# A four-layer graph network on one core: the weighted layer's sorted scan of gathered rows replaced by dense weight matrices of 144 sources

## The reference

```
h = relu(layernorm(x));  x = x + edge_statistics(h, edge_attr_32)      # sums, maxima, means over src, two matmuls
h = relu(layernorm(x));  x = x + convolution(h)                        # sums of scaled h[src] over dst, one matmul
h = relu(layernorm(x))
w = where(src != dst, edge_weight, 0)
x = x + (1 + eps) * h + segment_sum(w[:, None] * h[dst], src)          # the weighted layer
h = relu(layernorm(x));  x = x + gated(h, edge_attr_64, src, dst)      # two rounds of a GRU
```

## Time and profile before

| | us |
|---|---|
| median of 3 runs | 6442.04 (6427.77 to 6444.42) |
| span of the profiled execution | 6441.6 |
| median of the runs less that span | 0.4 |
| PE busy | 3666.2 (57%), 27862 instructions |
| DVE busy | 4108.0 (64%), 11121 |
| ACT busy | 1238.9 (19%), 3929 |
| POOL busy | 3600.3 (56%), 3398 |
| mean granted TensorE clock | 0.685 |

### The profile page before, as it was taken

How to read it: one execution, slowest core, us unless ns; L and a number is a source line. 1 busy time by engine, 2 the same in 40 slices (tenths; PEclk the granted TensorE clock), 3 DMA queues, 4 the chain that set the end, 5 groups by cost and what they waited for, 6 DMA issues and landing times. The chain is left out here.

```text
span 6441.6 us, 115669 instructions
## 1 busy us (share of the span) xinstructions
PE 3666.2 (57%) x27862; PEld 2870.0 (45%) x27863; DVE 4108.0 (64%) x11121; ACT 1238.9 (19%) x3929; POOL 3600.3 (56%) x3398
## 2 busy tenths in 40 slices
PE   4377778778778778740017686554432222210988
PEld 3234555555555555530017686554432222210977
DVE  8888877777777777769630577775554444432333
ACT  0023444444444444420010000000000000000111
POOL 0025777777777777740230277777777777763000
PEclk5588887887888887865559655555555555555999
DMA  1001211211111211127509344443333233321977
GB/s 25 2 20 35 63 53 51 63 53 52 61 54 52 63 53 52 61 78 286 182 17 426 108 99 100 102 95 78 87 76 71 58 69 69 69 50 62 386 292 269
DMA packets 459644, 634.91 MB, mean 99 GB/s; under 512 B 342019, under 2 KB 397479, under 8 KB 426087
## 3 DMA queue, kind: packets, MB, share of 16 engines
q1 hardware_dynamic: 347202, 493.86, 23.4%
q0 software_dynamic: 106624, 86.11, 6.5%
q10 hardware_dynamic: 5670, 53.26, 2.2%
HBM read 420.15 MB, written 212.81 MB: 98 GB/s over the span
## 5 line engine op out<-in xcount | busy, mean ns | idle before, releaser
L414 POOL DMA_INDIRECT sorted_rows<-rows,place_i x1568 | 1813.7, 1157 | 801.3 <-issue 462.6
L1349 POOL DMA_INDIRECT gathered_rows<-feature_table,gather_index x1568 | 1579.3, 1007 | 501.5 <-issue 463.0
L1435 PE MATMUL block_total<-attr_half,block_hot 128*128 128x65 f32 x4048 | 876.2, 418 | 320.0 <-DMA attr_half<-in_edge_attr_dram 304.5
L1435 PEld LDWEIGHTS block_total<-attr_half,block_hot 128*128 128x128 f32 x4048 | 867.2, 332 | 329.0 <-issue 309.9
L595 PE MATMUL part<-high,low 128*128 x3520 | 916.8, 392 | 118.3 <-DVE high L466 109.7
L466 DVE TENSOR_TENSOR high<-iota_g,window_keys 128x1568 f16 x880 | 850.8, 967 | 0.3
L580 PE MATMUL count_rows<-counts,lo_rows_f 128*128 128x49 f32 x3136 | 718.5, 320 | 0.0
L1393 DVE TENSOR_SCALAR block_hot<-iota_f,block_keys 128x128 f32<-128x128 f32 x2024 | 502.7, 302 | 183.5 <-PE block_total L1435 61.4
L595 PEld LDWEIGHTS part<-high,low 128*128 x3520 | 379.6, 108 | 484.9 <-issue 347.9
L580 PEld LDWEIGHTS count_rows<-counts,lo_rows_f 128*128 128x128 f32 x3136 | 579.5, 230 | 25.2 <-issue 21.0
L1404 DVE TENSOR_TENSOR_SCAN gathered_rows<-same_src,sum_carry,gathered_rows 128x32 f32<-128x32 f32 x3136 | 578.2, 266 | 6.3
(11 more groups left out here) (352 smaller groups left out, 5510.7 us busy)
## 6 DMA issues: line engine op xcount, KB each, us to landing
piece_round<-slabs SPq DMA_DIRECT2D x98, 1568.0 KB, 9.1
slabs<-slab SPq DMA_DIRECT2D x49, 1568.0 KB
piece_conv<-slabs SPq DMA_DIRECT2D x49, 1568.0 KB, 23.0
attr_half<-in_edge_attr_dram SPq DMA_DIRECT2D x184, 352.0 KB
scanned<-scan_out ACTq DMA_DIRECT2D x8, 6272.0 KB, 29.7
scanned<-gathered_rows SPq DMA_DIRECT2D x49, 1024.0 KB, 5.1
scan_rows<-sorted_rows SPq DMA_DIRECT2D x8, 3430.0 KB, 29.6
sorted_rows<-rows,place_i POOLq DMA_INDIRECT x1568
```

The lines of the kernel that those rows point to most:

```text
L414: pool.indirect_dma_start(sorted_rows[:, :], bass.IndirectOffsetOnAxis(ap=place_i[:, h, u:u + 1], axis=0), rows[:, h, u, :], None).then_in ...
L1349: pool.indirect_dma_start(got[b][:, j, :], None, table[:, :], bass.IndirectOffsetOnAxis(ap=index[b][:, j:j + 1], axis=0)).then_inc(gathere ...
L1435: nc.tensor.matmul(total[b][:, :], hot[:, j, :], attr[j // HALF][:, j % HALF, :], start=False, stop=True, skip_group_check=True).then_inc( ...
```

## The change

`sdw` and the sorted rows get a fourth column: src, a key, dst's low seven bits, and the weight, which is set to 0 where src equals dst. The key is made by fifteen more DVE operations in `prepare_keys`. `scan_sorted` drops its three operations for `dst_sorted` and `w_sorted`, and ACT copies the last three columns to `edge_records` in DRAM, sorted by source, 12 bytes per edge. `find_ranges` drops the blocks of 128 targets. Under the first layer, `edge_statistics_layer` writes the starts of the runs to DRAM, reads them back by group, and works out a plan: one pass per 128 edges of the fullest window of a group, with the first record of each window (`pass_index`) and the key base (`pass_base`) of each pass.

The table, the 1568 gathers and the 2024 one-hot products of the attributes go. In their place:

The core of the new code (in this order: the order of passes; ScalarE; VectorE; TensorE):

```diff
+        def passes(engine, name, body, between=None):
+            body(0, 0, None, 0)
+            body(1, 1, None, 1)
+            with engine.Fori(0, SCANS) as i:
+                for b in range(2):
+                    body(2 * i + 2 + b, b, 2 * i + b, 2)
+            if between is not None:
+                between()
+            count = one_value(nc, g["pass_count"][0:1, 0:1], name, LEAST, MOST)
+            with engine.Fori(SCANS, count) as i:
+                for b in range(2):
+                    body(2 * i + 2 + b, b, None, 2)
...
+            def second(q, b, j):
+                act.wait_ge(equal_ready, q * NBATCH + j + 1)
+                for w in range(GB):
+                    last = nc.scalar.mul(low[1][j % 2][:, w // 2, :, w % 2], equal[j % 2][:, w // 2, :, w % 2],
+                                         second_f[b][:, j * GB + w:j * GB + w + 1])
+                last.then_inc(second_made, 1)
+            def body(q, b, scan, since):
+                second(q, b, 1)
+                act.wait_ge(agg_ready, q + 1)
+                for n in range(4):
+                    copy(q, b, n)
+                second(q, b, 2)
+                for n in range(4, 8):
+                    copy(q, b, n)
+                second(q, b, 3)
+                for n in range(8, 12):
+                    copy(q, b, n)
+                if since:
+                    copy_agg(q - 1, 1 - b)
+                for n in range(12, 16):
+                    copy(q, b, n)
...
+            def batch(q, b, j):
+                k = j % 2
+                dve.wait_ge(bank_ready, q * BANKS + 4 * j - 4 + AHEAD)
+                if j == 0:
+                    dve.wait_ge(keys_ready, q + 1)
+                nc.vector.tensor_tensor(equal[k][:, :, :, :], iota(P), pair_keys(row[b], j, P), ALU.is_equal
+                                        ).then_inc(equal_ready, 1)
+                nc.vector.tensor_tensor(high[k][:, :, :, :], iota(KEYS), pair_keys(column[b], j, KEYS), ALU.is_equal)
+                dve.wait_ge(equal_ready, q * NBATCH + j + 1)
+                if j == 0:
+                    nc.vector.tensor_tensor(low[1][k][:, :, :, :], equal[k][:, :, :, :], pair_keys(second_w[b], j, P),
+                                            ALU.mult)
+                nc.vector.tensor_tensor(low[2][k][:, :, :, :], equal[k][:, :, :, :], pair_keys(third_w[b], j, P), ALU.mult)
+                nc.vector.tensor_tensor(low[0][k][:, :, :, :], equal[k][:, :, :, :], pair_keys(first_w[b], j, P),
+                                        ALU.mult).then_inc(made, 1)
...
+            def body(q, b, scan, since):
+                batch(q, b, 0)
+                batch(q, b, 1)
+                if scan is not None:
+                    scans(scan, b, 0, D // 2)
+                batch(q, b, 2)
+                take_keys(q + 1, 1 - b)
+                if scan is not None:
+                    scans(scan, b, D // 2, D)
+                batch(q, b, 3)
+                if scan is not None:
+                    keep_carry(scan, b)
...
+            def build(q, j):
+                k = j % 2
+                pe.wait_ge(made, q * NBATCH + j + 1)
+                if j:
+                    pe.wait_ge(second_made, q * (NBATCH - 1) + j)
+                for n in range(4):
+                    pe.wait_ge(bank_copied, q * BANKS + 4 * j + n + 1)
+                    for w in range(3):
+                        pair, side = divmod(3 * n + w, 2)
+                        for part in range(3):
+                            last = nc.tensor.matmul(bank[n][:, w * KEYS:(w + 1) * KEYS], low[part][k][:, pair, :, side],
+                                                    high[k][:, pair, :, side], start=part == 0, stop=part == 2,
+                                                    skip_group_check=True)
+                    last.then_inc(bank_ready, 1)
...
+                for a in range(first, last):
+                    side = a % 2 * D
+                    end = nc.tensor.matmul(ps_agg[b][side:side + D, 0:CSRC], h[:, a, :], dense[b][:, a, :], start=False,
+                                           stop=True, skip_group_check=True)
...
+            def body(q, b, scan, since):
+                build(q, 0)
+                build(q, 1)
+                turn(q + 1, 1 - b)
+                if since:
+                    apply(q - 1, 1 - b, 0, 24)
+                build(q, 2)
+                if since:
+                    apply(q - 1, 1 - b, 24, NB)
+                build(q, 3)
```

More of the change, by code:

```diff
@@ L616, in _, with scan_sorted @@
                             window(i, (h * RG + u) // 2, before)
[L619 removed]
+def scan_sorted(nc, g, sorted_rows, scanned, carries, records):
     J = 196
@@ L883, in _ @@
[L883 to L889 removed]
+            table = g["win_table"]
@@ new lines, in _ @@
+            pool.sem_inc(agg_added, 3)
+            pool.iota(offset_i[:, :], pattern=[[KEYS, CW]], base=0, channel_multiplier=0).then_inc(consts, 1)
+            for b in range(2):
+                pool.memset(rec[b][:, :, :], 0.0).then_inc(blank, 1)
+            pool.wait_ge(blank, 2)
+            for b in range(2):
+                fetch(b, b)
+            pool.memset(agg[:, :], 0.0).then_inc(cleared, 1)
+            pool.wait_ge(cleared, 1)
+            last = passes(pool, POOL, body)
+            add(last, 1)
@@ L1362, in _ @@
+            act.sem_inc(bank_copied, 4)
+            act.sem_inc(agg_copied, 3)
+            last = passes(act, ACTE, body)
+            copy_agg(last, 1)
         @block.vector
         def _(dve):
-            for b in range(2):
-                nc.vector.memset(attr[b][:, :, D:D + 1], 1.0).then_inc(consts, 1)
-            nc.vector.tensor_copy(iota_f[:, :], g["iota"][:, 0:P]).then_inc(consts, 1)
-            nc.vector.tensor_scalar(base[:, :], g["iota"][:, 0:NB], float(P), None, ALU.mult).then_inc(consts, 1)
@@ new lines, in scans @@
+            def scans(k, b, first, last):
+                if first == 0:
+                    dve.wait_ge(attr_in[b], (k - b) * 8 + 16)
+                    dve.wait_ge(carry_ready, k + 1)
+                for f in range(first, last):
+                    end = nc.vector.tensor_tensor_scan(got[b][:, :, f], same_dst[:, bass.ds(k * J2, J2)], got[b][:, :, f],
+                                                       carry[:, f:f + 1], ALU.mult, ALU.add)
+                if last == D:
+                    end.then_inc(scans_done, 1)
@@ L1419, in _ @@
+            nc.vector.memset(carry[:, :], 0.0).then_inc(carry_ready, 1)
+            step(nc.vector.tensor_copy(iota_2[:, :, :], g["iota"][:, 0:KEYS].unsqueeze(2).broadcast_to([P, KEYS, 2])))
+            dve.wait_ge(consts, 1)
+            step(nc.vector.tensor_copy(offset[:, :], offset_i[:, :]))
+            take_keys(0, 0)
+            passes(dve, DVE, body, between)
         @block.tensor
         def _(pe):
-            pe.sem_inc(used, HGRP)
-            pe.wait_ge(rest_in, 16)
-            pe.sem_inc(copied, U)
@@ L1471, in weighted_layer @@
+            pe.sem_inc(bank_ready, AHEAD)
+            pe.sem_inc(agg_ready, 2)
+            turn(0, 0)
+            last = passes(pe, PE, body, between)
+            apply(last, 1, 0, NB)
+def weighted_layer(nc, ctx, g, records, scanned, carries, dst, eps, edge_attr_64):
+    agg = ctx.enter_context(nc.sbuf_tensor("weighted_agg", [P, NCH * CSRC], F32))
+    g["attr_sum"] = agg[:, 0:NB * (D + 1)]
     with Scope(nc) as keep:
```

798 lines of the change are left out of this document (547 added, 251 removed).

## The result

The changed kernel takes 5724.28 us, median of 4 runs (5719.35 to 5728.72), against 6443.23 (4 runs, 6427.77 to 6447.89): ratio 0.8886, 95% interval 0.8874 to 0.8899. Its profiled execution has a span of 5720.5 us; forecast were 5716.

What follows compares the result with a forecast made beforehand. POOL's gather issue was taken to bound the weighted layer. Its replacement, 30 + 1351 (loops) + 15 + 142 = 1538 us against 2264, saves 726, elsewhere 0: 6441.6 - 726 = 5716 us, range 5660 to 5900 (5640 with rival 2).

Steps and rivals of the forecast that it cites:

- Scanning passes, 31.1 us, 995 in all: Weighted layer's 32 passes with an attribute scan: set by DVE's work, 31.1 us each, with PE's 22.3 us under it.
- Apply, 12.3 us: PE's apply step in each pass: 98 float32 matmul instructions at 125 ns each, 12.3 us.
- rival 2: The apply step's two column halves run side by side: apply 6.2 us, 70 us less, 5646 us in all; chance 0.12.
- Other passes, 23.7 us, 332 in all: The 14 passes without a scan: set by PE's 22.3 us plus 1.4 us of stall before build 1.
- Branch back, 20 us: Branch back of the large loop body: between 0 and 1.8 us, times 22; the middle, 20 us, was taken.
- tail: After the loops: the last apply step, 12.3 us, with its copy and addition, 15 us.
- Start, 30 us: New work before the loops: dst loads (7 us), copy and passes, locating runs, first gather and keys; 30 us with the barrier.
- End, 142 us: Layer's end: the same 98 gathers, 142 of the old 146 us, with DVE's 35 us of work hidden in their wait.
- Elsewhere, 0: Outside the weighted layer: key preparation +19 us, ranges -10.5, sorted scan -10, iota 1.5, pass plan hidden; together 0.
- rival 1: PE at 1.2 GHz sets the scanning passes' pace: 362 us more, 6078 us; chance 0.10.
- Rival 3: Products of one-hot and weight part run at one element a cycle, 1.67 for 0.873 us: 5959 us; chance 0.05.
- Rival 4: Handover waits make DVE and PE take turns, a pass 53.4 or 39.3 us: 6648 us, slower than before; chance 0.03.

Runs made afterwards that it cites:

- run 2: Changed kernel with 8 of a scanning pass's 64 scans moved from behind batch 1 to between batches 0 and 1: 5692.3 us, ratio 0.8826.
- run 1: Changed kernel with all 49 float32 multiplications of the apply step writing to PSUM partitions 0 to 63, instead of alternating halves: 5792.7 us.
- run 3: Changed kernel with DVE making the second weight part's products for all four batches and ACT for none: 5768.9 us.
- run 8: Changed kernel with 8 scans before batch 1, dst loaded early, second products by ACT (scanning passes: all; others: batches 2 and 3): 5663.3 us.
- run 10: Changed kernel with the first 24 of the apply step's 49 blocks moved from behind build 1 to between builds 0 and 1: 5716.4 us, ratio 0.8874.
- run 11: Changed kernel with 12 scans before batch 1, early dst, transfers cut at 112 rows, run 8's products and run 10's order: 5719.8 us, ratio 0.8858.
- run 6: Changed kernel with the 36 matmuls of each build issued as 72, each bank's parts twice over, same sums: 5944.4 us.
- run 4: Changed kernel with the three loads of dst issued at the start of the layer norm before: 5710.9 us.
- run 9: Changed kernel with 4 scans a pass instead of 64, and transfers of 125 or 124 rows cut into 112 and the rest: 5347.3 us.

## Why the prediction was right

The forecast was 5716 and the profiled execution took 5720.5. The sum is near, but several misses cancel in it, so each step is checked here:

- *Scanning passes, 31.1 us, 995 in all.* Right in mechanism and in every price; measured 31.8, 1018. Missed was DVE's wait for build 3 (1.3 us a pass, run 2): the forecast had put that stall into the other passes only, and took build 3 at full clock, where it took 3.9 to 4.6 us. Run 1 shows that with build 3 at full clock there is no such wait.
- *Apply, 12.3 us.* Mis-sized: 6.3. The step that failed is the price of 125 ns, taken from matmuls on one side; rival 2's mechanism, given 0.12, is what runs (run 1). In the scanning passes PE idles under the scans either way.
- *Other passes, 23.7 us, 332 in all.* Measured 20.3, 284. PE has 17.1 us of work for 22.3 (18.3 in every second pass, by the clock), but a stall of 2.8 for 1.4, since ACT's products take 0.293 us and not 0.204: the price "0.905 ns an element" from copies did not carry to a scaled product of 128. Rival 2's passes, DVE's 17.0 us plus a stall (5646 in all), failed on the same. PE with its gap (19.9 or 21.1) and ACT (18.4) lie 1.5 to 2.7 us apart: relieving one alone (runs 3, 8, 10) brought 0 to 0.3 us a pass over the whole loop, relieving both 2 us (run 11).
- *Branch back, 20 us.* No run shows the term: two passes make one round of the loop, and scanning ones differ by at most 0.8 us from one to the next, those of run 11 without a scan not at all; the 1.2 us by which the changed kernel's passes without a scan differ are build 1's clock. Taking the middle of a range from zero cost 20 us. (Only run 6, with its longer body, has a gap near the start of a round, its cause open.)
- *Between the loops* 8 for 4 us, *tail* 19.5 for 15. Loops and tail: 1330 for 1366, -36.
- *Start, 30 us.* Measured 44.4. The step that failed is "two loads of dst, 1.6 MB, some 7 us": 18 us from h to the cast, with a wait of 15.3 that goes when they are issued earlier (run 4) and falls to 6.8 with the transfers cut (run 9). +14.
- *End, 142 us.* 153, +11. The step that failed is the cover, "DVE's work on the new sums and the general round, some 35 us, lies in the 121 us wait": it ends long before the wait does, but from the first to the last of the 98 gathers it is 134.5 us, before 124.3, and the memset and the comparison of the general round fall together with 9.6 us of longer issues. The same stands in the traces of runs 4 and 9; no run leaves these operations out.
- *Elsewhere, 0.* +14. The sorted scan gained 9.5 us and the ranges 11.4, near the forecast. Key preparation cost 24.7 for 19, of which 1.3 is a later landing of the first loads: three operations that write or read every fourth float took 2.9 to 3.0 us, not 1.83, and three casts into every fourth float 1.6. The first layer, under whose gathers the pass plan lies, took 4.4 us longer, and its gathers too have longer issues beside DVE's operations, 6.7 us for 3.1. Counting the sources (+5.3), ranking (+4.5) and the convolution (-4.2) should not have changed, and why they did is open.

```profile
46.70 1.79 DVE L243 SCALAR_TENSOR_TENSOR over<-third,src_f 128x1568 f32<-128x1568 f32 x1
48.52 2.93 DVE L244 SCALAR_TENSOR_TENSOR sdw<-part_i,over 128x1568 f32<-128x1568 int32 x1
```

The sum: -36 + 14 + 11 + 14 + 2 (the gated layer) = +5. The time is inside the range of 5660 to 5900 by mechanism, since DVE's 31.1 us held; that 5716 is so near 5724 is luck. Two small things in the prediction's working: its 17.0 us for DVE without a scan holds 0.3 for a carry that these passes don't have, and rival 1's 362 us go by 42.4 us a pass, where PE's sum is 41.8.

*Rival 1*, PE at 1.2 GHz: half a truth. The scanning passes' builds behind a scan did fall to the lower level for all or part of their length (3.7 to 4.6 us for 36), the mean stayed at 0.82, and with some 10 us in which PE idles it cost 1.3 us a pass and not 11.3; in the passes without a scan it cost 1.2 us in every second one. The Trainium skill's warning (TensorE: Matmul & The Clock Gate, Loop structure matters more than you think) holds here for single bursts, not for the stage. *Rival 3*, products at one element a cycle: 0.87 us each, refuted. *Rival 4*, the handover: not in the change, but run 11 shows how near it is: two reorderings made DVE wait 2.6 us a pass for a step that both had put later.

## What to carry to other kernels

Once one engine is full, look for the bound just under it before counting on the gap: here attribute transfers at 27 us lay under DVE's 31.1 and ACT's 18.4 us under the 20.3 us of the passes without a scan, and they held the pace only once the first bound was gone. A price for an operation holds for its engine, its size and its place: copies did not price scaled products, nor one side of the array both, nor 128 rows 125. Work that lies under another engine's wait is hidden only if it leaves that engine's own work alone: here POOL's issues took longer beside it. And reorder for one kind of pass at a time: a step moved to fill a gap is late for whoever reads it in the other kind.

## What was not expected of the hardware

- Float32 matmuls with 64-column weights on alternating halves, one instruction in 65 ns; on one half 127 ns.
- Transfers of 125 rows of 12.8 KB: 119 GB/s for a load and a store together, DMA share 0.30; cut at 112 rows they no longer set the pace of a 21 us pass (share 0.50), and a store alone took 7.0 us for 14.3.
- More work for PE made most DVE-bound passes faster by 1.1 us (run 1): build 3 at the higher clock ends 1.4 us earlier.
- A gather that POOL issues while DVE is in a long operation took 3.4 to 7.6 us for 0.96 (beside a memset of 2.67, float32 operations of 3.48 and 6.83), in each of the traces looked at; nothing else made one of the 98 long.
- ScalarE: 0.293 us for a product of 128 bfloat16 elements at every second place with a scale per partition, as against 0.11 and 0.32 us for copies of 24 and 256 floats.
